# Quantised FFN of a two-layer kernel: down products between the next gates, magnitudes of three tiles taken on ScalarE, products 1024 wide

## The reference

```python
def fake_quant_nvfp4(x, global_scale):
    xb = x.reshape(sh[:-1] + (sh[-1] // BLOCK, BLOCK))
    amax = jnp.max(jnp.abs(xb), axis=-1, keepdims=True)
    sc = jnp.clip(amax / FP4_MAX * global_scale, 0.0, FP8_MAX)
    sc8 = sc.astype(jnp.float8_e4m3fn).astype(jnp.float32)
    dq = sc8 / global_scale
    safe_dq = jnp.where(dq == 0.0, 1.0, dq)
    a = jnp.clip(jnp.abs(xb) / safe_dq, 0.0, FP4_MAX)
    q = jnp.sign(xb) * _FP4_VALS[jnp.digitize(a, _FP4_MIDS)]
    return (q * dq).reshape(sh)
...
gate_out = nvfp4_linear(x, gate_w, s_in[0])
up_out = nvfp4_linear(x, up_w, s_in[0])
hidden = jax.nn.silu(gate_out) * up_out
return nvfp4_linear(hidden, down_w, s_in_down[0])
```

## Time and profile before

| | us |
|---|---|
| median of 3 runs (lowest to highest) | 811.29 (810.11 to 814.16) |
| the profiled execution | 815.65 |
| its span in the trace | 813.9 |
| DVE busy, share of the span | 613.4 (75%) |
| ACT busy | 378.6 (47%) |
| PE busy | 633.7 (78%) |

### The profile page before, as it was taken

How to read it: one execution, slowest core, us unless ns; L and a number is a source line. 1 busy time by engine, 2 the same in 40 slices (tenths; PEclk the granted TensorE clock), 3 DMA queues, 4 the chain that set the end, 5 groups by cost and what they waited for, 6 DMA issues and landing times.

```text
span 813.9 us, 13995 instructions
## 1 busy us (share of the span) xinstructions
PE 633.7 (78%) x3935; PEld 461.8 (57%) x3944; DVE 613.4 (75%) x1551; ACT 378.6 (47%) x674; POOL 210.3 (26%) x256
## 2 busy tenths in 40 slices
PE   5496867439999999958798999999655666675675
PEld 3383646316776667647687888887522333233333
DVE  5284657776666566677798889888759999999996
ACT  1241313013332333246455676665784667565562
POOL 6527362624455544410111222201100000000000
PEclk9598897759999999998899999999966889878978
DMA  8884443353221211060000000000000000000001
GB/s 322 266 303 148 147 137 123 105 153 146 61 69 48 65 54 51 26 209 1 1 0 0 0 0 0 0 0 2 2 3 0 14 13 26 26 13 13 25 26 53
DMA packets 30958, 53.99 MB, mean 66 GB/s; under 512 B 4973, under 2 KB 23806, under 8 KB 29760
## 3 DMA queue, kind: packets, MB, share of 16 engines
q1 hardware_dynamic: 24480, 39.02, 14.5%
q0 software_dynamic: 5568, 13.61, 4.8%
q10 hardware_dynamic: 864, 0.82, 0.3%
HBM read 39.38 MB, written 15.93 MB: 68 GB/s over the span
## 4 chain that ended last, share of the span: by engine, by line
PE 46%; DVE 30%; issue 11%; ACT 4%; another core or an unknown queue 3%; DMA 2%; SPq 2%; DVEq 1%; POOL 0%; ACTq 0%; POOLq 0%
PE quad L1134 9%; PE bank L1151 8%; PE quad L1083 5%; PE bank L1271 4%; DVE ctxs L1837 3%; PE quad L1255 3%; DVE hh L2176 3%; PE quad L1445 2%; PE bank L1286 2%; PE quad L1436 2%; DVE ctxs L1848 2%; PE quad L1142 2%; DVE nS L1996 2%; DVE nM L2001 2%
## 5 line engine op out<-in xcount | busy, mean ns | idle before, releaser
L1134 PE MATMUL quad<-W1s,xts 128*128 x160 | 74.1, 604 | 0.1
L1151 PE MATMUL bank<-W2s,hidT 128*128 x320 | 72.5, 379 | 0.3 <-ACT hidT L729 0.3
L1151 PEld LDWEIGHTS bank<-W2s,hidT 128*128 128x128 f32 x320 | 60.0, 190 | 12.6 <-issue 5.3
L605 POOL TENSOR_TENSOR X<-fo,X 128x256 f32<-128x256 f32 (+1 forms) x32 | 21.9, 684 | 168.5 <-DVE fo L2018 154.9
L1271 PE MATMUL bank<-nVB,nPT 128*128 128x34 f32 x512 | 63.0, 279 | 0.0
L1271 PEld LDWEIGHTS bank<-nVB,nPT 128*128 128x128 f32 x512 | 59.6, 191 | 3.7
L1468 PE MATMUL bank<-dT,hqT 128*128 128x256 bf16 x256 | 44.3, 333 | 22.3 <-ACT hqT L986 22.1
L725 ACT ACTIVATE hid<-hid 128x512 f32<-128x512 f32 x40 | 25.3, 633 | 75.4 <-DVE hid L1754 75.4
L554 POOL DMA_INDIRECT x_after_ffn<-row,niU x40 | 39.4, 985 | 69.6 <-DVE row L1766 51.8
L1754 DVE TENSOR_TENSOR hid<-quad,b1s 128x512 f32<-128x512 f32 x40 | 27.7, 692 | 34.2 <-PE quad L1134 27.9
L2176 DVE SCALAR_TENSOR_TENSOR hh<-quad,gmx,sil 128x512 f32<-128x512 f32 x64 | 45.3, 745 | 10.3 <-PE quad L1445 6.4
(11 more groups left out here) (322 smaller groups left out, 1475.5 us busy)
## 6 DMA issues: line engine op xcount, KB each, us to landing
row<-rows_by_expert SPq DMA_DIRECT2D x38, 134.0 KB
W1s<-in_ctxO SPq DMA_DIRECT2D x4, 1024.0 KB, 7.9
ctxs<-in_ctxT SPq DMA_DIRECT2D x4, 1024.0 KB
W1s<-in_W SPq DMA_DIRECT2D x8, 512.0 KB
W2s<-in_W SPq DMA_DIRECT2D x8, 512.0 KB
out<-yo SPq DMA_DIRECT2D x16, 256.0 KB, 2.1
X<-x_after_ffn SPq DMA_DIRECT2D x7, 516.0 KB, 6.8
b1s<-in_b SPq DMA_DIRECT2D x1, 2048.0 KB
```

The source lines that it names most:

```text
L1134: ins = pe.matmul(bank[2 + u % 2][:], xt[:, u, c, :], W1s[:, bass.ds(ex, 1), c, :].rearrange("p o s -> p (o s)"), start=c == 0, stop=c == ...
L1151: ins = pe.matmul(bank[6 + u % 2][:, 0:D], hidT[:, u % 2, c, :], W2s[:, bass.ds(ex, 1), c, :].rearrange("p o s -> p (o s)"), start=c == 0, ...
```

## The change

1. ACT's `hidden_size` becomes two functions: `hidden_half` is the copy to `hb` as before, and `hidden_size` writes the absolute value of the same elements to `absh` (1024 elements, an ACTIVATE with Abs). The first three tiles of a group get both; the fourth gets the copy alone. DVE's bitwise and over the hidden tiles shrinks from 4096 elements to the last tile's 1024. `s_ah` counts seven a group.
2. `tile_norm` writes the rows' absolute values to `absx` on ACT, and DVE's bitwise and over the rows goes.
3. DVE's `product` is one instruction of 1024 elements in place of two of 512. It waits for both halves of silu and of up, and frees both up banks at its end.
4. PE's transposes and downs of a group stand between the gates and ups of the next, and ACT's copies `hidden_out` between its silus. The tiles 2 and 3 of a group use the banks of 0 and 1, with the waits for that.

```diff
--- before.py
+++ after.py
@@ -778,6 +778,7 @@
                                          bias=nm2[:, bass.ds(t, 1)], scale=rs2[:, bass.ds(t, 1)])
                 ins.then_inc(s_x4, 1)
                 act.wait_ge(s_x4, g + 1)
+                act.activation(absx[g0 % 2], top(x4s[g0 % 2]), ACT.Abs)
                 act.copy(xb[g0 % 2], top(x4s[g0 % 2])).then_inc(s_ax, 1)
 
             def done_roots(part):
@@ -966,9 +967,16 @@
                     act.activation(sil[:, u % 2, k * 512:(k + 1) * 512], bank[2 + k][:], ACT.Silu,
                                    scale=gmx[:, 8:9]).then_inc(s_sil, 1)
 
+            def upper(u):
+                return top(hh[u // 2][:, (u % 2) * FF:(u % 2 + 1) * FF])
+
+            def hidden_half(t, u):
+                act.wait_ge(s_h, 2 * t + 2)
+                act.copy(hb[:, u * FF:(u + 1) * FF], upper(u)).then_inc(s_ah, 1)
+
             def hidden_size(t, u):
                 act.wait_ge(s_h, 2 * t + 2)
-                act.copy(hb[:, u * FF:(u + 1) * FF], top(hh[u // 2][:, (u % 2) * FF:(u % 2 + 1) * FF])).then_inc(s_ah, 1)
+                act.activation(absh[:, u * FF:(u + 1) * FF], upper(u), ACT.Abs).then_inc(s_ah, 1)
 
             x_out(0)
             tile_norm(1, 1)
@@ -976,32 +984,39 @@
             for u in range(4):
                 silu(u, u, first=u < 2)
                 if u:
-                    hidden_size(u - 1, u - 1)
-            hidden_size(3, 3)
+                    hidden_half(u - 1, u - 1)
+            for u in range(3):
+                hidden_size(u, u)
+            hidden_half(3, 3)
             act.wait_ge(s_nm2, 5)
             tile_norm(2, 2)
 
             def hidden_out(g, u):
                 act.wait_ge(s_hT, g * 4 + (u + 1))
-                act.copy(hqT[:, u % 2].rearrange("p c t -> p (c t)"), bank[(6, 0, 6, 6)[u]][:].bitcast(BF16)).then_inc(s_hTe, 1)
+                if u >= 2:
+                    act.wait_ge(s_dn, g * 4 + (u - 1))
+                act.copy(hqT[:, u % 2].rearrange("p c t -> p (c t)"), bank[(6, 0)[u % 2]][:].bitcast(BF16)).then_inc(s_hTe, 1)
 
             def group(i, i0, norm=True):
                 t = i * 4 + 4
                 x_out(i + 1)
                 silu(t, 0)
+                hidden_out(i, 0)
                 silu(t + 1, 1)
+                hidden_out(i, 1)
+                hidden_half(t, 0)
+                silu(t + 2, 2)
                 hidden_size(t, 0)
-                silu(t + 2, 2)
+                hidden_half(t + 1, 1)
+                silu(t + 3, 3)
                 hidden_size(t + 1, 1)
-                silu(t + 3, 3)
+                hidden_half(t + 2, 2)
                 hidden_size(t + 2, 2)
-                hidden_size(t + 3, 3)
-                hidden_out(i, 0)
-                hidden_out(i, 1)
+                hidden_half(t + 3, 3)
+                hidden_out(i, 2)
+                hidden_out(i, 3)
                 if norm:
                     tile_norm(i + 3, i0 + 3)
-                hidden_out(i, 2)
-                hidden_out(i, 3)
 
             NGR = NTILE // 4
             assert NGR % 2 == 0
@@ -1453,45 +1468,56 @@
                 up(u, u, first=u == 0)
             def hidden_in(i, u):
                 pe.wait_ge(s_hq, i * 2 + (u // 2 + 1))
+                if u >= 2:
+                    pe.wait_ge(s_hTe, i * 4 + (u - 1))
                 for c in range(FT):
-                    ins = pe.transpose(bank[(6, 0, 6, 6)[u]][:].bitcast(BF16)[:, c * P:(c + 1) * P],
+                    ins = pe.transpose(bank[(6, 0)[u % 2]][:].bitcast(BF16)[:, c * P:(c + 1) * P],
                                        hq[u // 2][:, ((u % 2) * FT + c) * P:((u % 2) * FT + c + 1) * P], identb[:])
                 ins.then_inc(s_hT, 1)
 
-            def down(i, u, turn=False):
+            def down(i, u, first=False):
                 pe.wait_ge(s_hTe, i * 4 + (u + 1))
-                if turn:
-                    hidden_in(i, 3)
-                if u == 0:
-                    pe.wait_ge(s_y, i * 4)
+                if u % 2 == 0 and not first:
+                    pe.wait_ge(s_y, i * 4 + (u - 2))
                 for c in range(FT):
                     ins = pe.matmul(bank[(1, 7)[u // 2]][:, (u % 2) * D:(u % 2 + 1) * D], hqT[:, u % 2, c, :], dT[:, c, :],
                                     start=c == 0, stop=c == FT - 1)
                 ins.then_inc(s_dn, 1)
 
-            def ahead(i):
+            def ahead(i, first=False):
+                t = i * 4 + 4
                 pe.wait_ge(s_xqe, i + 2)
-                for u in range(4):
-                    gate(i * 4 + (4 + u), u)
-                    up(i * 4 + (4 + u), u)
-
-            def finished(i):
+                gate(t, 0)
+                up(t, 0)
                 hidden_in(i, 0)
+                gate(t + 1, 1)
                 hidden_in(i, 1)
-                down(i, 0)
+                up(t + 1, 1)
+                gate(t + 2, 2)
+                down(i, 0, first)
+                up(t + 2, 2)
+                down(i, 1)
+                gate(t + 3, 3)
+                up(t + 3, 3)
+                finished(i, first)
+
+            def finished(i, first=False):
                 hidden_in(i, 2)
-                down(i, 1)
-                down(i, 2, turn=True)
+                hidden_in(i, 3)
+                down(i, 2, first)
                 down(i, 3)
 
             NGR = NTILE // 4
             x_in(1)
-            ahead(0)
+            ahead(0, first=True)
             with pe.Fori(0, NGR - 2) as k:
-                finished(k)
+                pe.wait_ge(s_hTe, k * 4 + 4)
                 x_in(k + 2)
                 ahead(k + 1)
-            finished(NGR - 2)
+            hidden_in(NGR - 1, 0)
+            hidden_in(NGR - 1, 1)
+            for u in range(2):
+                down(NGR - 1, u)
             finished(NGR - 1)
 
 
@@ -1859,12 +1885,11 @@
 
             def rows_sizes(g, g0, steps):
                 v.wait_ge(s_ax, g + 1)
-                steps.link(ts(absx[g0 % 2].bitcast(I16), xb[g0 % 2].bitcast(I16), 0x7FFF, None, ALU.bitwise_and))
                 halves(absx[g0 % 2], halfx, 16, NBX // 16, big[:, rows_c], steps)
 
             def hidden_sizes(g, steps):
-                v.wait_ge(s_ah, g * 4 + 4)
-                steps.link(ts(absh.bitcast(I16), hb.bitcast(I16), 0x7FFF, None, ALU.bitwise_and))
+                v.wait_ge(s_ah, g * 7 + 7)
+                steps.link(ts(absh[:, 3 * FF:].bitcast(I16), hb[:, 3 * FF:].bitcast(I16), 0x7FFF, None, ALU.bitwise_and))
                 halves(absh, halfh, 4, NBH // 4, big[:, hid_c], steps)
 
             def rows_scaled(g0, steps):
@@ -2169,12 +2194,10 @@
 
             def product(t, u):
 
-                for k in range(2):
-                    v.wait_ge(s_sil, 2 * t + (k + 1))
-                    v.wait_ge(s_um, 2 * t + (k + 1))
-                    o = (u % 2) * FF + k * 512
-                    v.scalar_tensor_tensor(hh[u // 2][:, o:o + 512], bank[4 + k][:], gmx[:, 11:12],
-                                           sil[:, u % 2, k * 512:(k + 1) * 512], ALU.mult, ALU.mult).then_inc(s_h, 1)
+                v.wait_ge(s_sil, 2 * t + 2)
+                v.wait_ge(s_um, 2 * t + 2)
+                v.scalar_tensor_tensor(hh[u // 2][:, (u % 2) * FF:(u % 2 + 1) * FF], quad[:, 2:4].rearrange("p k f -> p (k f)"),
+                                       gmx[:, 11:12], sil[:, u % 2], ALU.mult, ALU.mult).then_inc(s_h, 2)
 
             def results(g, ks=(0, 1)):
                 for k in ks:
@@ -2218,7 +2241,7 @@
                 product(u, u)
             group(0, 0, False)
             with v.Fori(0, (NTILE // 4 - 2) // 2) as i:
-                st.enter(i, 46)
+                st.enter(i, 44)
                 group(i * 2 + 1, 1, True)
                 group(i * 2 + 2, 2, True)
                 st.leave((NTILE // 4 - 2) // 2)
```

## The result

The changed kernel takes 825.06 us (median of 4 runs, 819.98 to 829.46), the one before 810.7 us (809.15 to 814.16). The ratio is 1.0174 with a 95% interval of 1.0118 to 1.0231. The forecast was 821 us, in a range of 809 to 828.

A forecast was written before the change was run, and what follows sets the result against it. DVE bounds the steady part before; afterwards ACT's queue, with PE at the lower clock, sets the period. Six groups +6.7, first tiles +2.8, end +0.8, start -0.4 give +9.9 us, 811.29 to 821, range 809 to 828.

The forecast's parts named there:

- The bound before and what DVE saves: Steady groups: DVE bounds at 26.08 us; savings of 0.46, 0.81 and 0.52 would leave DVE alone needing 24.3.
- ACT's chain, 11.98 us: Steady group: ACT runs without a gap from the first `hidden_out` to the end of the fourth tile's copy, 11.98 us.
- The period as T + 20.9: Steady group's length; T runs from the end of `xq` to the end of the first transposes of `hq`.
- The clock and T: Group start: PE at the lower clock until about the first transposes, T = 6.3, period 27.2 us, +6.7 over six groups.
- The first rival: Steady groups: PE's clock stays up or returns before the first up, T = 4.6, period 25.5, total 809 us; chance 0.16.
- The third: Steady groups: clock returns only with the second up, T about 6.75, +14 in all, 825 us; chance 0.24.
- it idles some 4 us where it idled 2.90, then 4.5 more: PE's waits in a steady group: some 4 us for ACT's copies, some 4.5 more before `xq`; hence the lower clock.
- First four tiles: Start of the stage: later first product and copies move the maxima from 608.17 to 610.5; taken as +2.8 us.
- Start and end: Rows quantised ahead of the stage -0.4 us; last group's maxima +1.7 and the very end -0.9, sum +0.8.
- The rule that spoke against the change: Skill page advises VectorE over ScalarE for plain arithmetic; ACT pays 3.8 us a group for 1.3 of DVE's.

The follow-up runs named there:

- e5: Changed kernel with unread matmuls filling PE's two waits and five more between `x_in` and the gates; ratio to before 1.0012, five filled groups at 25.55 us.
- e6: Kernel before with part 4 (the weave) alone, products of 512, no Abs on ACT; ratio to before 1.0074, mean period 27.40 us.
- e3: Changed kernel with part 4 (the weave) undone, all four Abs and the wide product kept; ratio to before 0.9983, mean period 25.37 us.
- e7: Kernel before with the weave alone plus unread matmuls in PE's waits; ratio to before 0.9979, mean of five filled groups 26.0 us.
- e2: Changed kernel with the three tiles' absolute values back on DVE, the rows' Abs left on ACT; ratio to before 1.0109, period 27.45 us.
- e1: Changed kernel with part 3 undone, each product again two instructions of 512; ratio to before 1.0145, mean period 27.47 us.
- e4: Changed kernel with unread matmuls filling PE's two waits, none between `x_in` and the gates; ratio to before 1.0080, mean period 26.44 us.
- n_two_tiles: Kernel before, its PE order and products of 512, with the rows' and two tiles' absolute values on ACT; 785.07 us against 791.54, ratio 0.9912.
- n_three_tiles: n_two_tiles with a third tile's absolute value on ACT; ratio to before 0.9977, mean period 25.52 us.
- n_two_tiles_busy: n_two_tiles with 10 unread matmuls ahead of `x_in` and 5 ahead of the gates; ratio to before 0.9973, mean period 26.03 us.

## Why the prediction was right, step by step

- **The bound before and what DVE saves: right.** The product of 1024 took 1284 ns on average, forecast 1.27; the and of 1024 0.43 busy.
- **ACT's chain, 11.98 us: right,** 12.0 measured. An Abs of 1024 took 1.06 to 1.11 us, a trifle over the copy's 1.05; its share of the queue is the 0.94 that was used. There is no further table load.
- **The period as T + 20.9: right,** in all 24 steady groups of four kernels to 0.02 us.
- **The clock and T: the mechanism right, the size a little low.** T was taken as 6.3 and measured as 6.46 in the group shown; the periods lie between 27.32 and 27.55 for a forecast of 27.2. That is 1.4 us more than forecast over six groups. `x_in` and the first gate and up ran at the lower clock, 1.2 GHz. The first rival (clock up) is what e5 shows and what the changed kernel does not do. The third (a late return) gave 825 us, which is the measured time, but its mechanism did not come: it had the second gate of each steady group at 1.2 GHz, and the measured one was at 2.4 (1.03 for four matmuls in the group from 704.78).
- **What I had not seen:** the forecast made ACT's added work and its order the cause, and the clock a condition. By e6 the kernel before with nothing but the weave has the same 27.4, with DVE late in place of ACT. The Abs and the wide product neither add to the steady loss nor take from it as long as PE is slow at the start of a group; they gain 0.7 us a group once the weave is gone (e3). So the steady loss begins at one step of the working, "it idles some 4 us where it idled 2.90, then 4.5 more": with that idle time filled, e5 and e7 have 25.55 and 25.8.
- **First four tiles: mis-sized,** +3.8 for +2.8. The forecast took 1.03 us for each up, and one at the lower clock as the bound of +3.2. The second gate and the second up each took 1.89 and the third gate 1.44. Taking back the tiles' Abs gives 0.6 of the 3.8 (e2), and taking back these, the rows' Abs and the wide product all of it (e6). What the wide product alone makes is open, since in e1 the clock came back earlier as well.
- **Start and end: wrong in size.** For the rows ahead of the stage DVE's work is 0.4 us shorter, as forecast, but PE's `x_in` followed 1.69 us after that `xq` where it had been 1.28, and that took it back. In e4 and e5, whose program is the changed kernel's up to there, it is 1.64 and 1.40, so this may be no more than the difference of two executions. In the last group the maxima came 1.8 us later after `xq`, forecast 1.7, and what follows them was 1.8 shorter, forecast 0.9. The sum is 0.0 where +0.8 was forecast.
- **Luck.** The profiled execution is 13.8 us longer for a forecast of 9.9. The rest is, up to rounding, 2.4 ahead of the stage, most of it not the change's, 1.0 in the first four tiles and 1.4 in the steady groups, less 0.8 at the end. So part of the distance to the forecast, and the agreement of the median with the third rival's 825, is chance.
- **The rule that spoke against the change.** An absolute value of 1024 elements takes 0.43 us on DVE and 1.06 on ACT, and yet with ACT 37% idle n_two_tiles gains by moving it there. The Trainium skill, "ScalarE: Activation LUTs", section "Rules for kernel authors", prefers VectorE for simple functions such as relu, max or add; the busy times of the absolute value agree with that, the kernel's time here does not. Abs and Silu alternate without a load between them. The same page of the Trainium skill, section "Table sets: the hidden batching unit", has abs in every set, and the trace agrees.

## What to carry to other kernels

Weaving finished work into the next round moves it out of a gap, and on this engine the gap is not free: look what fills the time just ahead of the critical first matmuls, because here a PE that had waited 4.5 us there started them at half speed. Work moved from the bound engine to an idle one is worth its busy time only if its place in that engine's queue lies behind nothing that the bound engine waits for, and what stands behind it moves too. An edit that takes work from a late chain and gives it to one that is almost as late can leave the time as it was (e2) and says nothing of the cause; undo the shared cause, or put one part alone into the kernel before.

## What the runs showed of the hardware

PE's clock was low at `x_in` (1.03 for eight transposes) behind waits of 4.5 to 8.1 us. In e4 it was at 2.4 GHz at `x_in` (0.62) and at 1.2 at the gate (1.89), behind waits of 1.24 and 1.21 us with only eight transposes between them; two other groups of e4 with the same waits had fast gates, so these waits alone do not tell which comes. With five matmuls in the second of these gaps it stayed at 2.4 GHz in all five groups of e5. In n_two_tiles the downs reach to the next `xq`, the wait at `x_in` is 0.47 or none in most groups, and the gates behind the same 1.22 us are fast without filling; where it was 2.43, the gate took 1.89. In n_three_tiles `x_in` was at the lower clock (1.06) with no wait ahead of it, behind sixteen downs that took 3.62. When the clock comes back differs between executions of the same program: in n_two_tiles the second gate of the first four tiles took 1.89 us and in n_two_tiles_busy 1.18, and their first parts differ by 1.8 us.
